# A decoder layer on one core: the second attention pass with its keys on the partitions

## The reference, cut to what matters

```
x   = x + mamba(rmsnorm(x))                 # in_proj, conv, softplus, selective scan with 16 states, gate, out_proj
x   = x + swiglu(rmsnorm(x)); x = layernorm(x)
q   = x Wq + bq;  k = ctx Wk + bk;  v = ctx Wv + bv          # 16 heads of 32, 64 keys
a1  = softmax(q k / sqrt(32))               # first pass: per head its maximum, its entropy, the mean score
T   = exp(clip(mlp(mean score, mean maximum, entropy)))      # one temperature per head and batch element
a2  = softmax(q k / (2 T))                  # second pass: the attention that is used
x   = layernorm(x + (a2 v) Wo + bo)
g   = top-2 gates of softmax(x R);  x = layernorm(x + x W + b + sum_e g_e (x A_e) B_e)
```

## Time and profile before

| what | value |
|---|---|
| median of the timed runs (3) | 4237.48 us (4236.95 to 4242.27) |
| profiled execution | 4236.39 us, span 4234.6 us |
| PE busy | 3678.8 us, 87% |
| DVE, ACT, POOL busy | 2507.1, 2173.1, 2491.3 us |
| mean granted PE clock | 0.911 |

### The profile page before, as it was taken

How to read it: one execution, slowest core, us unless ns; L and a number is a source line. 1 busy time by engine, 2 the same in 40 slices (tenths; PEclk the granted TensorE clock), 3 DMA queues, 4 the chain that set the end, 5 groups by cost and what they waited for, 6 DMA issues and landing times.

```text
span 4234.6 us, 36098 instructions
## 1 busy us (share of the span) xinstructions
PE 3678.8 (87%) x9848; PEld 1746.2 (41%) x9848; DVE 2507.1 (59%) x3319; ACT 2173.1 (51%) x5186; POOL 2491.3 (59%) x1100
## 2 busy tenths in 40 slices
PE   6555999799979998999989998999989999999577
PEld 3111433343434345554334335554334435554254
DVE  2676378747774886248774786347774787322211
ACT  3453445554565556455556457365556457341543
POOL 0999199819982996119981997209990998200000
PEclk9555999899989998999989999999989999999788
DMA  4333245324433452125442443225442443112000
GB/s 151 109 115 112 84 159 161 128 93 152 165 123 105 151 167 97 63 75 179 157 134 79 160 159 115 70 61 171 156 138 79 151 162 132 55 55 80 10 30 20
DMA packets 221267, 483.17 MB, mean 114 GB/s; under 512 B 31884, under 2 KB 32268, under 8 KB 220812
## 3 DMA queue, kind: packets, MB, share of 16 engines
q1 hardware_dynamic: 221068, 480.87, 34.8%
HBM read 470.82 MB, written 9.96 MB: 114 GB/s over the span
## 4 chain that ended last, share of the span: by engine, by line
PE 44%; POOL 5%; DVE 5%; ACT 5%; issue 3%; POOLq 0%; ACTq 0%; DVEq 0%
PE ps L1490 24%; PE ps L1579 4%; PE ps L1591 4%; POOL hb L961 4%; PE ps L1548 3%; DVE hb L1296 2%; PE ps L1624 2%; POOL hb L951 2%; PE ps L1658 1%; PE ps L1670 1%; ACT ps L1171 1%; PE ps L1687 1%; PE ps L1700 1%; PE ps L1541 1%; PE ps L1651 1%
## 5 line engine op out<-in xcount | busy, mean ns | idle before, releaser
L951 POOL TENSOR_TENSOR hb<-dtu,bc 128x1024 f32<-128x1024 f32 x512 | 1206.4, 2358 | 114.1 <-PE ps L1591 77.8
L961 POOL TENSOR_TENSOR hb<-hb,bc 128x1024 f32<-128x1024 f32 x512 | 1206.7, 2357 | 97.0 <-issue 45.8
L1490 PE MATMUL ps<-fT,wden 128*128 128x512 f32 x2304 | 1037.9, 598 | 17.5 <-DVE hm L1334 6.0
L1010 ACT ACTIVATE ps<-dt,a_neg 128x512 f32<-128x512 f32 x1024 | 691.3, 689 | 641.1 <-DVE hb L1296 635.6
L1591 PE MATMUL ps<-hb,ident 128*128 128x512 f32 x1024 | 621.1, 698 | 277.5 <-POOL hb L961 275.1
L1490 PEld LDWEIGHTS ps<-fT,wden 128*128 128x128 f32 x2304 | 438.4, 192 | 572.5 <-issue 569.2
L1296 DVE TENSOR_TENSOR_SCAN hb<-ps,state,hb 128x512 f32<-128x512 f32 x512 | 626.7, 1266 | 34.8 <-ACT ps L1010 21.7
L1296 DVE TENSOR_TENSOR_SCAN hb<-ps,hb 128x512 f32<-128x512 f32 x512 | 595.8, 1205 | 16.0 <-POOL hb L951 10.6
L1305 DVE TENSOR_TENSOR ps<-ps,hb 128x512 f32<-128x512 f32 x512 | 355.6, 695 | 377.2 <-POOL hb L961 376.1
L1579 PE MATMUL ps<-wden,hm 128*128 128x512 f32 x1024 | 478.2, 613 | 13.8 <-DVE res L1350 10.2
L1490 PE MATMUL ps<-xnT,wmix 128*128 128x512 f32 x1024 | 464.3, 603 | 10.1 <-ACT xnT L1034 7.8
(11 more groups left out here) (193 smaller groups left out, 3891.7 us busy)
## 6 DMA issues: line engine op xcount, KB each, us to landing
bc<-bc_dram SPq DMA_DIRECT2D x1024, 256.0 KB, 3.5
wden<-in_w SPq DMA_DIRECT2D x192, 512.0 KB, 3.6
wmix<-in_w_mix SPq DMA_DIRECT2D x96, 512.0 KB, 3.6
watt<-in_w_qof SPq DMA_DIRECT2D x32, 512.0 KB, 4.4
xm<-in_x SPq DMA_DIRECT2D x8, 1024.0 KB, 5.3
res<-in_x SPq DMA_DIRECT2D x8, 1024.0 KB, 6.6
wden<-in_w_qof SPq DMA_DIRECT2D x16, 512.0 KB, 3.9
out<-res SPq DMA_DIRECT2D x8, 1024.0 KB, 4.4
```

The lines of the kernel that those rows point to most:

```text
L951: TTn(hb[:, k % 4], dtu[:, :, :], bc[:, 0, k % 3].unsqueeze(1).broadcast_to([P, 2, CH]), ALU.mult).then_inc(s.s1_ready, 1)
L961: TTn(hb[:, k % 4], hb[:, k % 4], bc[:, 1, k % 3].unsqueeze(1).broadcast_to([P, 2, CH]), ALU.mult).then_inc(s.s3_done, 1)
L1010: A_(dst, dt[:, p % 2, jj], ACT.Exp, scale=a_neg[:, j, n:n + 1]).then_inc(full_of(key), 1)
L1490: ins = M(dst, a, b, start=start and n == 0, stop=stop and n == len(pairs) - 1)
```

## The change

1. Second pass. A unit sc2 now has the keys of a pair of heads stationary and 256 queries (two tiles) moving, for two pairs; a second product of 16 rows adds the negative row maximum, which a new unit `shift` has turned and copied to `mxT`. ACT takes the exponential of 256 columns at a time with the temperature as a scale per partition, in place in the bank, and copies the bank with a Relu to `at`. The turning (flip) is gone. The values' block has two more columns, with ones for the keys of either head, so the product gives the sums as well; it is done in two halves, each in a bank of its own, and DVE clamps, inverts and multiplies.
2. Keys and values become units of `y` behind chunk 0's projection, with wk, wv and the bias held in `res` and `hm` for the time being; x is loaded first, then the 14 constants, then the first mixer weights, the context, wk, wv and the bias.
3. The planner's dense banks grow from four to eight once the last `turn_out` is done. `PHASE` has one value per chunk, and `WORK` and `LOOK` are other numbers.
4. Values are loaded into one block instead of two alternating ones, after the last value product of the batch element before.

```
 def y_plan():
-    got = []
+    got = [("key", 0, c4) for c4 in range(KC)] + [("value", 0, b) for b in range(BATCH)]
...
-        got.append(("ent", c))
+        got += [("ent", c), ("shift", c)]
...
     for c in range(CHUNKS):
-        def e2(t, hf):
-            return [("e2", c, t, hf, 0), ("e2", c, t, hf, 1)]
-        got += [("sc2", c, 0, 0), *e2(0, 0), ("sc2", c, 0, 1), *e2(0, 1)]
-        for t in range(TT):
-            more = t + 1 < TT
-            got += [("flip", c, t, 0), ("flip", c, t, 1)] + ([("sc2", c, t + 1, 0)] if more else [])
-            got += [("val", c, t), ("on", c, t)] + ([("sc2", c, t + 1, 1), *e2(t + 1, 0)] if more else [])
-            got += [("fl2", c, t)] + (e2(t + 1, 1) if more else []) + [("wo", c, t), ("woa", c, t)]
+        for q in range(TT // 2):
+            got += [("sc2", c, q, 0), ("sc2", c, q, 1), ("e2", c, q, 0), ("sc2", c, q, 2), ("e2", c, q, 1), ("sc2", c, q, 3),
+                    ("e2", c, q, 2), ("e2", c, q, 3)]
+            for t in (2 * q, 2 * q + 1):
+                got += [("val", c, t), ("on", c, t)] + ([("wo", c, t - 1), ("woa", c, t - 1)] if t % 2 else []) + [("fl2", c, t)]
+            got += [("wo", c, 2 * q + 1), ("woa", c, 2 * q + 1)]
...
+    if kind == "key":
+        part(PE, 2 * MM, ("proj", 0), takes=(u,))
+        part(ACT_, 0.5, mine(), gives=(u,))
+    elif kind == "value":
+        part(PE, 4 * MM, ("proj", 0), takes=(u,))
+        part(DVE, EV, mine(), gives=(u,))
...
     elif kind == "temper":
-        part(DVE, 2.3, ("clip", c), ("e2", c - 2, last, 1, 1), gives=(("mlp", c),))
+        part(DVE, 0.3, ("clip", c), ("e2", c - 2, 1, 3), gives=(("mlp", c),))
+    elif kind == "shift":
+        part(PE, 0.5, ("ent", c), ("sc2", c - 2, 1, 3), takes=(u,))
+        part(ACT_, EV, mine(), gives=(u,))
     elif kind == "sc2":
-        part(PE, TURN, ("temper", 2 * b + 1), takes=(u,))
+        part(PE, 2.2 * MM, ("temper", 2 * b + 1), ("shift", c), ("val", c, 2 * i - 1) if i else ("val", c - 1, last), takes=(u,))
     elif kind == "e2":
-        part(ACT_, 2.5, ("sc2", *u[1:4]), ("flip", c, i - 1, u[3]) if i else ("lora", c - 1), ("val", c, i - 2),
-             gives=(("sc2", *u[1:4]),) if u[4] else ())
-    elif kind == "flip":
-        part(PE, 0.65, ("e2", *key, 1), takes=(u,))
-        part(ACT_, EV, mine(), ("val", c, i - 1), gives=(u,))
+        part(ACT_, 1.6, ("sc2", *key), ("fin", c - 1, last), gives=(("sc2", *key),))
     elif kind == "val":
-        part(PE, 1.7, ("flip", c, i, 0), ("flip", c, i, 1), takes=(u,))
+        part(PE, 2.4, ("e2", c, i // 2, 3), takes=((*u, 0), (*u, 1)))
     elif kind == "on":
-        part(DVE, 1.0, ("val", *key), ("fl2", c, i - 1), gives=(("val", *key),))
+        part(DVE, 1.5, ("val", *key), ("fl2", c, i - 1), gives=(("val", *key, 0), ("val", *key, 1)))
...
-WORK = {"x": 176.0, "s": 103.0, "y": 304.0}
-PHASE = {"y": (6.12, 6.26), "s": (7.49, 7.0), "x": (9.46, 7.8)}
+WORK = {"x": 145.0, "s": 103.0, "y": 304.0}
+PHASE = {'y': (5.956, 6.26, 6.109, 6.26, 6.12, 6.26, 6.12, 6.275), 's': (7.32, 7.013, 7.5, 7.019, 7.5, 7.032, 7.418, 7.313), 'x': (9.363, 7.845, 9.439, 7.668, 9.278, 7.207, 9.133, 7.538)}
...
-            if not free:
+            if len(free) < len(p[5]):
                 return None
-            t = max(t, min(free.values()) + HOP)
+            t = max(t, sorted(free.values())[len(p[5]) - 1] + HOP)
...
+            if u == ("turn_out", CHUNKS - 1):
+                free.update({k: end for k in RING_F})
...
-LOOK = {"m": 0.25, "l": 0.1, "x": 0.09, "y": 0.3, "s": 0.3}
+LOOK = {'m': 0.231, 'l': 0.1, 'x': 0.049, 'y': 0.3, 's': 0.3}
...
+    kept = DONE[("value", 0, BATCH - 1)]
+    got += [(kept, 2, ("kv_store", 0)), (kept + 4, 2, ("kv_load", 0)), (kept + 5, 2, ("kv_load", 1))]
+    got.append((kept + 6, 2, ("v_load", 0)))
     for b in range(1, BATCH):
-        got.append((DONE[("woa", 2 * b - 3, TT - 1)] + 1 if b > 1 else 1.0, 2, ("kv_load", b)))
+        got.append((DONE[("val", 2 * b - 1, TT - 1)], 2, ("v_load", b)))
+    for b in range(2, BATCH):
+        got.append((DONE[("woa", 2 * b - 3, TT - 1)] + 1, 2, ("kv_load", b)))
...
+                if b:
+                    filled(sp, ("val", 2 * b - 1, TT - 1, 1))
                 vv = v_dram[b].rearrange("k (a e d) -> k a e d", e=2, d=DK)
                 for e in range(2):
-                    sp.dma_start(vbd[64 * e:64 * e + 64, r, :, DK * e:DK * e + DK], vv[:, :, e, :]
-                                 ).then_inc(kv_in[r], 16)
...
+                    sp.dma_start(vbd[64 * e:64 * e + 64, :, DK * e:DK * e + DK], vv[:, :, e, :]).then_inc(v_in, 16)
...
+            def store_kv():
+                for c4 in range(KC):
+                    emptied(sp, ("key", 0, c4))
+                for b in range(BATCH):
+                    emptied(sp, ("value", 0, b))
+                for c4 in range(KC):
+                    sp.dma_start(k_dram[:, c4].rearrange("b p k -> p b k"), kT[:, c4].rearrange("p (b k) -> p b k", b=BATCH)
+                                 ).then_inc(s.kv_stored, 16)
+                for b in range(BATCH):
+                    sp.dma_start(v_dram[b], vR[:, b]).then_inc(s.kv_stored, 16)
+                sp.wait_ge(s.kv_stored, 16 * 2 * BATCH)
+
             load_x(0)
...
+            sp.dma_start(ctxT, A["ctxT"].rearrange("p (c k) -> p c k", c=KC)).then_inc(s.ctx_in, 16)
+            sp.dma_start(res[:, 1], A["wk"]).then_inc(s.ctx_in, 16)
+            sp.dma_start(res[:, 2], A["wv"]).then_inc(s.ctx_in, 16)
+            sp.dma_start(hm[:, 1], A["bv"].partition_broadcast(P)).then_inc(s.ctx_in, 16)
...
+                nc.gpsimd.memset(vbd[64 * e:64 * e + 64, :, 2 * DK + e:2 * DK + e + 1], 1.0).then_inc(s.zeroed, 1)
...
+                elif kind == "key":
+                    A_(kT[:, i], filled(act, unit)[:, 0:BATCH * KEYS], ACT.Identity, bias=bk_c[:, i:i + 1]).then_inc(free_of(unit), 1)
...
+                    if c == 0 and i == 0:
+                        act.wait_ge(s.kv_stored, 16 * 2 * BATCH)
...
                 elif kind == "e2":
-                    hf, q = unit[3], unit[4]
-                    key = ("sc2", c, i, hf)
-                    bank = filled(act, key).rearrange("p (h k) -> p h k", k=KEYS)
-                    if q == 0:
+                    n = unit[3]
+                    bank = filled(act, ("sc2", c, i, n))
+                    if n == 0 and i == 0:
                         act.wait_ge(s.tempered, b + 1)
-                    if q == 0 and hf == 0:
-                        if i >= 2:
-                            emptied(act, ("val", c, i - 2))
-                        elif c:
-                            emptied(act, ("val", c - 1, TT - 2 + i))
-                    for h in range(4 * q, 4 * q + 4):
-                        hh = 8 * hf + h
-                        ins = A_(eb[:, hh], bank[:, h], ACT.Exp, bias=nm2[:, TT * half + i, hh:hh + 1],
-                                 scale=ftv[:, 0, hh:hh + 1], accum_out=den[:, 0, i % 2, hh:hh + 1])
-                    if q:
-                        ins.then_inc(free_of(key), 1)
-                elif kind == "flip":
-                    hf = unit[3]
-                    if hf == 0 and i:
-                        filled(act, ("val", c, i - 1))
-                    key = ("flip", c, i, hf)
-                    A_(at[:, hf * 512:(hf + 1) * 512], filled(act, key), ACT.Relu).then_inc(free_of(key), 1)
+                    for m in range(2):
+                        ins = A_(bank[:, m * 256:(m + 1) * 256], bank[:, m * 256:(m + 1) * 256], ACT.Exp,
+                                 scale=ftc[:, 2 * n + m:2 * n + m + 1])
+                    ch.link(ins)
+                    A_(at[:, 2 * n:2 * n + 2], bank.rearrange("p (m q) -> p m q", m=2), ACT.Relu
+                       ).then_inc(free_of(("sc2", c, i, n)), 1)
...
-
-                        for hf in range(2):
-                            emptied(dve, ("sc2", c - 2, TT - 1, hf))
-                    V.tensor_scalar(ftv[:, 0], tmp16[:, 3], 0.5, None, ALU.mult).then_inc(free_of(("mlp", c)), 1)
-                    ch.link(V.tensor_scalar(ftv[:, 1], tmp16[:, 3], -0.5, None, ALU.mult))
-                    V.tensor_tensor(nm2[:, :, :], mxs[:, :, :], ftv[:, 1].unsqueeze(1).broadcast_to([P, 8, HEADS]), ALU.mult
+                        for n in range(4):
+                            emptied(dve, ("sc2", c - 2, 1, n))
+                    V.tensor_scalar(ftc[0:64], tmp16[0:64, 3].rearrange("p (m e) -> p m e", e=2)[:, :, 0], 0.5, None, ALU.mult
+                                    ).then_inc(free_of(("mlp", c)), 1)
+                    V.tensor_scalar(ftc[64:128], tmp16[64:128, 3].rearrange("p (m e) -> p m e", e=2)[:, :, 1], 0.5, None, ALU.mult
                                     ).then_inc(s.tempered, 1)
                 elif kind == "on":
-                    key = ("val", c, i)
-                    src = filled(dve, key).rearrange("p (h d) -> p h d", d=DK)
-                    for hf in range(2):
```

(76 more changed lines are left out.)

114 lines of the change are left out of this document (46 added, 68 removed).

## The result

The changed kernel is slower: 4297.6 us (four runs, 4293.1 to 4303.5) against 4237.2 for the kernel before beside it, a ratio of 1.0144 [1.0126, 1.0162]. The forecast was 4174, with 4226 as the upper end. The profiled execution took 4296.8 us, its span is 4295.0.

What follows compares the result with a forecast made beforehand. POOL was taken to bound chunk 0's scan, PE the middle where two second passes run (shared with the scan elsewhere), latency the end. 4236.4 - 30 (start) - 12 (middle) - 20 (end) = 4174.4, said as 4174; 8-in-10 range 4100 to 4226.

Steps and rivals of the forecast that it cites:

- Part 1: Start: keys and values beside chunk 0 and x loaded first; 33.7 us earlier, less 4 leaked: -30 us.
- the leak: Chunk 0's scan: delays from key products, ACT copies, DVE adds and SP's queue; 4 us, bounds 0 to 20.
- Part 2: Second pass on PE: added subtracting products less the dropped turns, net +3.9 us per chunk.
- Part 3: Second pass on ACT and DVE: ACT relieved by 30 us a chunk, DVE +0.8 us a tile.
- Part 4: Middle: added PE work costs +23 us, a third of PE's idle time returns, -35: -12 us.
- A: Whole kernel: the forecast itself, 4174 us, own range 4150 to 4205; chance 0.45.
- C: Middle: the order does more, two thirds of 112 us come back, -52 net: 4134 us; chance 0.20.
- Rival B: Middle gives nothing back because PE is 93% busy there, +23 us: 4209 us; chance 0.22.
- Part 5: End: second passes of chunks 6 and 7 shorten by 8.5 and 6 us, extra banks give 5: -20 us.
- D: Until the end: PE waits for the four dense banks, 18 waits taken, +22 us: 4258 us; chance 0.09.
- E: Start: SP's queue delays the scan's rows and POOL starves; middle gives nothing: 4225 to 4232 us; chance 0.04.

Runs made afterwards that it cites:

- e3: Kernel before with only keys and values moved beside chunk 0 and x loaded first; old second pass, phases and four banks: 4208.6 us.
- e1: Changed kernel with the maxima-subtracting product over all 128 rows instead of 16, so it computes something else: 4189.1 us.
- e11: Kernel before with keys and values beside chunk 0 and the step-size product over 128 rows, old second pass: 4186.1 us.
- e14: Changed kernel made exact with subtracting and step-size products over 128 rows, and the planner settings of the kernel before: 4162.2 us.

## Why the prediction was wrong

**Part 1, -30: right.** Up to the end of scan 0 it is -28.3. The start is 35.8 us earlier (forecast 33.7), and the leak is 7.5 us (forecast 4): scan 0 took 320.0, over the 317 that I had named as its limit. e3 gave 4208.6 where the other parts at nothing make 4206.

**Part 2, the failed step.** It said "I take full price": 0.434 us for each 16-row product and nothing for what stands beside it, because the 64-row records' mean was "693 ns, not below the 598". I read the row as a floor. What it held was a surcharge: in order of time the steps beside a change of rows are 0.52 to 0.53 us against 0.429. The mean alone would not have proved it, since the 128-row records of L1591 have a mean of 698 in the same trace; the order in time does. The surcharge holds for the 16-row records and, which no row of mine priced, for both records of the full product between them. A unit of eight records takes 2.5 us instead of 1.73 at full clock, and 4.6 at half. The second thing that part 2 put at nothing is the clock, which falls in 10 of 15 blocks. Together they are the 108.5 us between the changed kernel and e1.

The Trainium skill, "TensorE: Matmul & The Clock Gate", section "Step-by-step: what each phase is for", has the time follow the moving columns. The traces agree between records of the same rows (0.429 us at 512 columns, over 128 rows and inside a run of 64 or 33) and not at a change of rows: at the same 256 columns the 16 rows took 4297.6 us and the 128 rows 4189.1. The prediction has the 64-row products side with that rule of the Trainium skill; most of their steps lie at a change, and those do not.

**Part 3, ACT: direction right, size wrong.** I added 110.9 us of accumulator reads to 199.0 of exponentials. The chain of waits of before has 27 such records in 5.24 us, 0.194 each: a pair takes 0.39, so the reads lie inside. ACT lost 147.6 us, 18.5 a chunk instead of 30. The same error is in part 4: a unit of four exponentials took 1.6 us, not 2.4, so the new unit, 1.4 us, is hardly shorter; there are 8 a chunk instead of 16.

**Part 4, middle, -12: the sign is right once the rows are full, the size is not.** It was +45.3 in the changed kernel; with 128 rows -25.6 (e1), and -26.5 between e11 and e14, with PE 5.7 us busier, where I had counted 23, and ACT 92.9 less. That lies between A (-12) and C (-52). No run shows that it is ACT's relief that pays, as part 4 argued. Rival B, nothing back (+23), is refuted for full rows.

**Part 5, end, -20: wrong with full rows too.** It was +43.4, and the end grew, which I had named as a sign of being wrong; e1 has +8.2 (617.5 us), e14 against e11 +0.3. Pass 6 of e14, from the chain of waits:

```profile
3934.63 1.15 PE ps L1640 x2
...
3944.67 0.82 ACT ps L1228 x2
3945.51 0.60 ACT xw L1231
3946.46 2.91 PE ps L1684 x16
3949.37 1.00 issue
3950.37 1.09 PE ps L1692 x4
3951.46 3.31 PE ps L1684 x16
3954.77 1.81 PE ps L1698 x2
3956.58 3.97 PE ps L1507 x8
...
3993.80 0.69 DVE res L1450
```

That is 59.2 us where I said 48.8; pass 7 takes 56.8 (4046.30 to 4103.11) where I said 46.6. The old pass takes 57.2 and 52.8 in e11. The block of scores takes 11.8 instead of 8.7, as PE comes to it from idling at 1.2 GHz. Two tiles take 19.8 and 18.8 instead of 15.7: the values' products take 2.91 and 3.31, not 2.0, and the output product 5.8, not 4.3. The clock again:

```profile
3946.40:3954.80 8.40, 7.34 (x37) 7.21 (x38) 2.37 (x9) 0.60 (x1) 0.00 (x0) 0.55 0.00 0
```

I had taken 1.96 from a tile whose values' product ran right behind dense records; the new order puts the first values' product of a tile pair behind a wait for ACT.

**The rivals.** D forecast slower, but by waits for banks, so it had the sign and not the cause. Its nearest row, PE's load waiting for DVE's row sums, fell from 24.7 us in nine waits to 10.9 in five. L1624 held the scores of both passes and L1654 holds those of the first alone; the keys' products of the second (L1639) wait 0.6 us in all for another engine:

```profile
PEld ps L1654 <- DVE se L1396: 10.9, 5, 3.0
```

E is refuted by the start. The miss of 123 us is 54.0 for the change of rows from 128 to 64 and 54.5 for going on to 16, with its clock. The 15 that are left are the miss of e1: in its profile the end is 28 us over the forecast, the middle 14 under it, the start 2 over. What stays open: why 16 rows let the clock fall where 64 didn't; whether the surcharge goes by the number of rows or by which rows they are, since no run changes one without the other; and how much of the order's 20 us steps belongs to which wait.

## What to carry to other kernels

A short contraction (a matmul over few rows) is not cheaper than a full one, and between full ones it costs more than they do. Count each change to fewer rows and back, put short ones behind one another, and if zeros can fill the rest of the 128 rows, fill them; filling was tested here, grouping was not. When a row that is to show "no discount" lies above its neighbour, look at its records in order of time and price the difference. Compare two algorithms only with an order drawn for each: here the order moved one and the same kernel by 20 us either way.

## What the runs showed of the hardware

- Between records of the same rows the step from start to start is 0.216 us at 256 columns (128 rows) and 0.429 at 512 (128, 64 and 33 rows). At a change of rows two steps are longer, the one across it (0.304 to 0.309 us; 0.519 to 0.523 at 512 columns) and the one behind it (0.320; 0.533), also where the record is a full one. The change costs the same with 16 rows as with 64. Filling the step-size product's rows took 14.0 us off the new pass and 22.6 off the old.
- The clock fell in a dense run of 16-row and 128-row records by turns, with PE never idle, in 10 of 15 blocks that started at 2.4 GHz; it fell in none of 15 in the same run with 64 rows, and in none with 128. Started at 1.2 GHz behind an idle PE, a block stayed there to its end with 16 and with 64 rows (20.3 us), and rose after 5.4 us with 128.
